# A twelve-layer Perceiver block in one program: a bias moved from GpSimd to ScalarE, weight splitting moved to two other layers, and one pair of weight loads put behind one more wait

## The reference

```python
# L0 attention (l0a below): 16 heads of 128, causal
# L0 feed-forward (l0f): Hadamard transforms around a gated MLP of 1024
# L1 attention (l1a): a state-space layer; for each row
v1, v2 = (v[..., 0::2], v[..., 1::2])       # v is B + B_bias, and C + C_bias, 64 heads x 64
c, s = (jnp.cos(phi), jnp.sin(phi))
r1 = v1 * c - v2 * s
r2 = v1 * s + v2 * c
# L2 feed-forward (l2f): mixture of experts, the two best of 8 by softmax score
# L3 cross-attention (l3x): fp8-rounded inputs against fp32 weights
y = jnp.clip(x.astype(jnp.float32) / scale, -FP8_MAX, FP8_MAX)   # then rounded to bf16, to fp8
q = _fp8_linear_pertensor(ln_out, wq, wq_scale, q_in_scale)      # also wk, wv, wqx
out = jnp.einsum('bsi,oi->bso', catq, wproj) * (proj_in_scale * proj_w_scale)
```

## Time and profile before

| | us |
|---|---|
| runs before (three) | 3519.94, 3521.09 (median), 3527.53 |
| the profiled execution | 3520.92 |
| its span in the profile | 3519.1 |
| PE busy | 2822.5 (80% of the span) |
| DVE busy | 2205.2 (63%) |
| ACT busy | 1477.5 (42%) |
| POOL busy | 755.1 (21%) |
| l0a | 410 to 757 |
| l0f | 757 to 889 |
| l1a | 1050 to 1507 |
| l2f | 2085 to 2254 |
| l3x | 2254 to 2925 |
| GpSimd idle within a round, l0f / l2f | 30.0 to 32.9 / 33.3 to 34.2 |
| a quarter of wproj in l3x, from issue to landing (median) | 8.8 |

### The profile page before, as it was taken

The page is one execution under the profiler, slowest core; times in us unless marked ns, Lnnn a source line. Parts: engine busy times, 40 slices in busy tenths (PEclk is TensorE's granted clock), DMA queues, the critical chain, the costliest instruction groups (busy, mean ns, idle before and its releaser), DMA issues. The chain is left out here.

```text
span 3519.1 us, 63930 instructions
## 1 busy us (share of the span) xinstructions
PE 2822.5 (80%) x24148; PEld 2008.9 (57%) x24148; DVE 2205.2 (63%) x4685; ACT 1477.5 (42%) x3000; POOL 755.1 (21%) x1074
## 2 busy tenths in 40 slices
PE   6777699978777788857998759788788886888687
PEld 3333387867664556534655336455555565777576
DVE  6999644542558888866565643376676774433764
ACT  4899611111446464534443113255455541332223
POOL 5222177400002232211111001121111112322100
PEclk8889799999887776758999879899889997999798
DMA  3999933200010000010000241112211124000000
GB/s 119 199 205 204 208 138 104 86 24 1 15 54 8 3 3 2 2 74 10 6 6 7 75 112 44 39 40 102 84 75 75 75 101 159 1 1 1 1 1 13
DMA packets 340727, 217.82 MB, mean 62 GB/s; under 512 B 298139, under 2 KB 318875, under 8 KB 332833
## 3 DMA queue, kind: packets, MB, share of 16 engines
q1 hardware_dynamic: 332260, 214.49, 22.3%
q10 hardware_dynamic: 8256, 0.52, 0.2%
HBM read 127.95 MB, written 18.87 MB: 42 GB/s over the span
## 5 line engine op out<-in xcount | busy, mean ns | idle before, releaser
L1252 ACT ACTIVATE l0x_pb<-l0x_ex,l0x_neg_max,l0x_q_scale 128x2048 uint16<-128x2048 f32 x128 | 267.1, 2088 | 36.5 <-POOL l0x_neg_max L1355 27.7
L1151 PE MATMUL l0x_s_ps<-l0x_kT,l0x_qT 128*128 128x512 bf16 x512 | 179.4, 443 | 76.1 <-DVE l0x_ex L1450 39.2
L1448 DVE TENSOR_SCALAR_CACHE_REDUCE l0x_ex<-l0x_s_ps 128x1024 f32<-128x1024 f32 x128 | 156.2, 1220 | 14.5 <-PE l0x_s_ps L1151 13.7
L1450 DVE TENSOR_SCALAR_CACHE_REDUCE l0x_ex<-l0x_s_ps 128x1024 f32<-128x1024 f32 x128 | 156.1, 1220 | 1.0 <-PE l0x_s_ps L1151 1.0
L264 PE MATMUL l3x_bank<-l3x_w_kv_x,l3x_ctxT 128*128 128x512 f32 x256 | 127.4, 644 | 8.4 <-ACT l3x_ctx_k L766 4.6
L1151 PEld LDWEIGHTS l0x_s_ps<-l0x_kT,l0x_qT 128*128 128x128 bf16 x512 | 35.0, 103 | 156.5 <-DVE l0x_ex L1450 104.0
L1161 PEld LDWEIGHTS l0x_o_ps<-l0x_v,l0x_vT 128*128 128x128 f16 x2048 | 71.5, 99 | 55.8 <-DMA l0x_vT<-l0x_pb 25.3
L2315 PEld LDWEIGHTS l1a_bank<-l1a_u,l1a_gm 64*64 64x64 f32 x2048 | 95.3, 193 | 13.5 <-issue 12.7
L2315 PE MATMUL l1a_bank<-l1a_u,l1a_gm 64*64 64x8 f32 x2048 | 98.0, 234 | 3.4 <-DVE l1a_gm L2671 3.3
L2307 PE MATMUL l1a_bank<-l1a_r,l1a_r 32*64 32x64 f32 x2048 | 72.6, 282 | 31.7 <-DVE l1a_r L2653 28.0
L3782 PE MATMUL l3x_bank<-l3x_wproj,l3x_cat 128*128 128x256 bf16 x768 | 90.8, 276 | 7.9 <-DVE l3x_cat L3668 7.9
(11 more groups left out here) (775 smaller groups left out, 7688.1 us busy)
## 6 DMA issues: line engine op xcount, KB each, us to landing
l3x_wproj<-l3x_wproj_parts SPq DMA_DIRECT2D x32, 1536.0 KB, 8.8
l3x_wproj_parts<-l0a_parts SPq DMA_DIRECT2D x24, 256.0 KB, 2.9
l0a_raw<-in_L_xattn_wproj SPq DMA_DIRECT2D x8, 512.0 KB, 4.5
l3a_w<-in_L_attn_W SPq DMA_DIRECT2D x4, 1024.0 KB, 11.4
l3x_wq_parts<-l0a_parts SPq DMA_DIRECT2D x12, 256.0 KB, 3.0
l3x_wqx_parts<-l0a_parts SPq DMA_DIRECT2D x12, 256.0 KB, 2.4
l3x_wq<-l3x_wq_parts SPq DMA_DIRECT2D x1, 3072.0 KB, 10.2
l3x_wqx<-l3x_wqx_parts SPq DMA_DIRECT2D x1, 3072.0 KB, 12.9
```

The costliest lines, as they stand in the source:

```text
L1151: ins = mm(s_ps[:, j * 512:(j + 1) * 512], qT[:, h, :], kT[:, h // 2, j * 512:(j + 1) * 512], start=True, stop=True)
L1252: s.activation(pb[:, h % 4, :], ex[:, h % 4, :], ACT.Exp, scale=q_scale[:, h:h + 1], bias=nb[:, h:h + 1], accum_out=sums[:, h:h + 1]).then ...
L1448: v.tensor_scalar(ex[:, h % 4, 0:1024], s_ps[:, 0:1024], 1.0, None, ALU.mult, ALU.max, accum_out=low_max[:, h:h + 1]).then_inc(o.up(scores ...
L1450: v.tensor_scalar(ex[:, h % 4, 1024:2048], s_ps[:, 1024:2048], 1.0, None, ALU.mult, ALU.max, accum_out=high_max[:, h:h + 1]).then_inc(o.up ...
```

## The change

Three edits.

One. `WeightParts` takes the projections or the output weights alone. The 12 chunks of the projections are now divided in l0f, three in each of its four rounds, behind the norms; the 8 chunks of wproj in l2f, two in each round, behind the second softmax power. SP's loads and stores move along: three chunks are asked for ahead of `load_next`, and the stores follow behind it. Layer l0a has none of it any more, and its GpSimd loop is a hardware loop.

Two. In l1a the bias of B is added by ACT, 16 instructions of 128x128 for each half, just ahead of C's; GpSimd adds none.

Three. In l3x SP waits for `kc1.filled` of the next tile as well before it issues quarters 0 and 1.

```diff
@@ WeightParts
-    def __init__(self, L, d):
+    def __init__(self, L, d, projections=(), output=False):
...
-        for kind, name in enumerate(("wq", "wk", "wv", "wqx")):
+        for kind, name in projections:
...
-        for n in range(8):
+        for n in range(8 if output else 0):
@@ l0a, SP and GpSimd
-            parts.load_first(sp)
             load_next(sp, env)
-            parts.store_all(sp)
...
-            for t in range(TILES - 1):
-                for j in range(3 * t, min(3 * t + 3, len(parts.chunks))):
-                    parts.divide(pool, j)
+            with pool.Fori(0, TILES - 1) as t:
                 o = Order(pool, L.order["pool"], t)
                 o.t = t + 2
                 whole(norm.pool(o))
@@ l0f, SP and GpSimd
+        parts = WeightParts(L, env.dram, projections=enumerate(("wq", "wk", "wv", "wqx")))
...
+            parts.load_first(sp)
             load_next(sp, env)
+            parts.store_all(sp)
...
-            in_turn(*(tile["gpsimd"](pool, 0) for tile in tiles))
-            with pool.Fori(1, TILES // 2) as t:
+            for t in range(TILES // 2):
                 in_turn(*(tile["gpsimd"](pool, t) for tile in tiles))
+                for j in range(3 * t, 3 * t + 3):
+                    parts.divide(pool, j)
@@ l1a, ACT
-            def biased_c(o, half):
-                for e, dst in enumerate((v1[1], v2[1])):
-                    for k in range(half * NG // 2, (half + 1) * NG // 2):
-                        last = e and k == (half + 1) * NG // 2 - 1
-                        s.activation(dst[:, k, :], vt[:, 2 + e, :], ACT.Identity, bias=bc_bias[:, 2 + e, k:k + 1]).then_inc(o.up(c_biased if last else None), 1)
+            def biased(o, half):
+                for n, biased_n in enumerate((b_biased, c_biased)):
+                    for e, dst in enumerate((v1[n], v2[n])):
+                        for k in range(half * NG // 2, (half + 1) * NG // 2):
+                            last = e and k == (half + 1) * NG // 2 - 1
+                            s.activation(dst[:, k, :], vt[:, 2 * n + e, :], ACT.Identity, bias=bc_bias[:, 2 * n + e, k:k + 1]).then_inc(o.up(biased_n if last else None), 1)
@@ l1a, GpSimd
-            def biased_b(o, half):
-                ks = slice(half * NG // 2, (half + 1) * NG // 2)
-                pool.wait_ge(vt_ready.sem, vt_ready.value(o.t))
-                if o is not first:
-                    pool.wait_ge(roped.sem, roped.value(o.t - 1, 3 if half else 1))
-                for e, dst in enumerate((v1[0], v2[0])):
-                    g_.tensor_tensor(dst[:, ks, :], vt[:, e, :].unsqueeze(1).broadcast_to([P, NG // 2, P]),
-                                     bc_bias[:, e, ks].unsqueeze(2).broadcast_to([P, NG // 2, P]), ALU.add).then_inc(o.up(b_biased if e else None), 1)
...
-                    for half in range(2):
-                        biased_b(o, half)
@@ l2f, SP and GpSimd
+        parts = WeightParts(L, env.dram, output=True)
...
+            parts.load_first(sp)
             load_next(sp, env)
+            parts.store_all(sp)
...
                 in_turn(*(tile["gpsimd"](pool, t) for tile in tiles))
+                for j in range(2 * t, 2 * t + 2):
+                    parts.divide(pool, j)
@@ l3x, SP
                     sp.wait_ge(y_ps.sem, y_ps.value(t))
+                    sp.wait_ge(kc1.filled.sem, kc1.filled.value(t + 1))
                     quarters(0, 1)
```

More of the change, by code:

```diff
@@ L1538, in load_first @@
     def load_first(self, sp):
-        sp.dma_start(self.scale[:], self.scale_src).then_inc(self.scale_loaded, 16)
+        if self.chunks[0][2]:
+            sp.dma_start(self.scale[:], self.scale_src).then_inc(self.scale_loaded, 16)
         for j in range(self.BUFFERS):
@@ L1606, in l0_attn @@
         y_ps, tile_done, x_biased = L.sig("y_ps"), L.sig("tile_done", primed=True), L.sig("x_biased")
-        parts = WeightParts(L, env.dram)
         block = L.block()
@@ L2464, in _ @@
             for half in range(2):
-                biased_c(first, half)
+                biased(first, half)
                 sines(first, half)
@@ L2484, in tile @@
                     act.wait_ge(roped.sem, roped.value(t, 1))
-                    biased_c(o, 0)
+                    biased(o, 0)
                     sines(o, 0)
                     act.wait_ge(roped.sem, roped.value(t))
-                    biased_c(o, 1)
+                    biased(o, 1)
                     sines(o, 1)
@@ L2541, in _ @@
             odd_steps_of(first, 1)
-            for half in range(2):
-                biased_b(first, half)
             def tile(t, more):
```

## The result

The changed kernel takes 3565.8 us in the median of four runs (3560.6 to 3570.7), against 3520.5 before: ratio 1.0123, 95% interval 1.0107 to 1.0140. Its profiled execution has a span of 3564.3 us, 45.2 over that of before. By stages, in us, from GpSimd's first layer norm (L231) of a layer to that of the next; l3x is counted from the norm named `l3x_ln`, 2.3 us behind its first.

| | before | after | difference | forecast |
|---|---|---|---|---|
| l0a | 331.2 | 314.1 | -17.1 | -16.5 |
| l0f | 133.2 | 149.2 | +16.0 | +14 |
| l1a | 478.6 | 543.8 | +65.2 | +60 |
| l2f | 171.2 | 187.4 | +16.2 | +28 |
| l3x | 665.1 | 625.6 | -39.5 | -54 |

The account below looks back on a forecast made before the run. No one engine was taken to bound the program, so each edit was priced in its own stage: -16.5 + 14 + 28 + 60 - 54 = +31.5 on 3520.9, giving 3552 us. Its own range was 3535 to 3569, the overall range 3509 to 3580.

Parts of the forecast that it names:

- the 3.5 taken from the first tile: l0a: of the first tile's 8.9 us over, 3.5 were expected back when splitting is taken out.
- The chain of the alternation: l0f, first round: 14 VectorE instructions alternate with GpSimd's, setup ends 22 us later where 6.3 were free: +14.
- 6 us, and 1 more for the clock: l2f: cost of a round from VectorE's held routing instructions and the clock behind idle time; 4 x 7 = +28.
- Six instructions were counted as held: l2f, second tile's routing: six of ten small VectorE instructions each wait for GpSimd, 7 to 9.5 us together.
- The step in VectorE's and ScalarE's chain: l1a: ScalarE's added 9.1 us a tile less 0.7 slack, less 1.1 from a quicker L2562: +7.3 a tile.
- 9 and one tile's 7.3: l1a: 9 us for the first tile's 32 added instructions, 7.3 for each of seven loop tiles; +60 in all.
- no issue time before L964: l3x: sign that the forecast is right, VectorE's issue wait of 7.04 us in a loop tile gone.
- Gain 45.1 + 6 x 1.3 = 53: l3x: L927's whole wait goes and six tiles' stretch to L820 shortens by 1.3 each; with 1 more, -54.
- The sentence on the Trainium skill's rule: l3x: a taken branch out of the window makes a DMA fetch, so part of the wait stays after the change.
- Rival B: VectorE's small and setup instructions not held by GpSimd: l0f +2, l2f 0, total 3512, faster; chance 0.14.
- Rival D: l1a's longer ScalarE run is absorbed: l1a +8 to +17, total about 3505; chance 0.06.
- Rival C: Quarters don't hold the fetch, or it meets them elsewhere: l3x gains 0 to half, 3579 to 3606; chance 0.12.

Follow-up runs that it names:

- run four: Kernel before with only the splitting moved to l0f and l2f, GpSimd also waiting there for VectorE's down weights and first expert product: 3516.7 us, ratio 0.9978.
- run two: Kernel before with one edit, quarters 0 and 1 of the next tile in l3x also waiting for kc1.filled: 3487.8 us, ratio 0.9894.
- run five: Kernel before with only quarter 1 in l3x waiting for kc1.filled, quarter 0 loaded where it was: 3508.4 us, ratio 0.9949.
- run six: Kernel before with VectorE's loop over tiles in l3x written out, so no jump back, quarters loading where they did: 3474.6 us, ratio 0.9860.
- run three: Kernel before with one edit, the splitting of the weights moved from l0a to l0f and l2f: 3539.5 us, ratio 1.0046.
- run eight: Kernel before with C's bias for the second half of the groups in l1a added by GpSimd, not ScalarE: 3534.1 us, ratio 1.0023.
- run nine: Kernel before with quarters later, one chunk left in l0a, eleven in l0f and eight in l2f behind VectorE's work, B's bias on GpSimd: 3469.1 us, ratio 0.9841.
- run ten: Kernel before with quarters later, splitting mostly moved behind VectorE's work, B's bias on GpSimd, and VectorE's l3x loop written out: 3460.7 us, ratio 0.9816.
- run seven: Kernel before with ScalarE adding B's bias in l1a for the second half of the groups only, GpSimd the first: 3553.1 us, ratio 1.0087.
- run one: Kernel before with one edit, B's bias in l1a on ScalarE and none on GpSimd: 3585.6 us, ratio 1.0184.

## Why the prediction was right, and where its sizes were off

The sign, the range and the mechanisms held: 3565.8 measured, 3552 forecast, in the forecast's own range of 3535 to 3569. That the total is so near is in part luck. Two stages were off by more than 10 us, one each way: l2f cost 12 less than forecast, and l3x gained 14.5 less. With only the error of l3x and those of l1a and l3a the total would have been about 3576, outside that range.

- l0a, -17.1 for -16.5: right, even the 3.5 taken from the first tile.
- l0f, +16.0 for +14: right. The chain of the alternation came as worked out: 14 instructions held, the setup 21 us later within its stage (22 forecast), and 15.1 of the 16 us are in the first round. Run four shows that the alternation is the cause: without it the setup is as short as before, and of its +8 in l0f 5.8 come from three chunks that begin behind the setup and end too late for the next norm.
- l2f, +16.2 for +28. The step that failed in size is "6 us, and 1 more for the clock" a round; it was 4.0. Six instructions were counted as held, each for 1.2 to 1.6 us. Four were, for 0.14, 1.76, 0.71 and 1.94 us; the two that came right behind a held one (L623, L628) went through. L681 came 4.1 to 4.6 us later in its round, and not 6 to 8. The cause is shown: run four takes the cost away by the order alone.
- l1a, +65.2 for +60. The step in VectorE's and ScalarE's chain was right: L2550 did take 0.55 us for 1.41, and VectorE waits for the scale. A loop tile is 7.7 us longer in the mean of six (6.6 to 8.3) and not 7.3; the first L2705 comes 18.2 us later, where 9 and one tile's 7.3 were forecast, and the last tile adds 1.3. Most of the excess is a wait that wasn't in the sum. The copy to vt comes 8.25 us behind dt_raw in the mean of seven tiles (8.23 in the tile shown, 1312.21 to 1320.44), and came 7.7 behind it before. VectorE stands idle between them for TensorE's L2308 in five of these tiles, for 0.4 to 2.0 us, before in two, for 0.4 and 0.6. TensorE's granted clock over l1a was 0.69 for 0.72; that this is why TensorE is late was not tried.
- l3x, -39.5 for -54. The cause was right, by runs two, five and six. One of the signs did not come: "no issue time before L964" held in all but two tiles. The step that was mis-sized is "Gain 45.1 + 6 x 1.3 = 53": it took the whole wait as gone and the last tile's 17.6 us from L927 to L820 as what a loop tile would get. 8.4 us of the wait stayed, since the fetch behind the jump takes time even with the quarters out of its way (run six). And the stretch shortened by 2.7 us in all and not by 8. TensorE's low clock did go: L927 takes 1.06 us for 1.94, and the granted clock from 2534 to 2560 is 1.00. But TensorE now waits 2.2 us in the stretch for ScalarE's rows (L759, four waits of 0.16 to 0.74), and ScalarE waits 2.8 and 2.6 us there for the keys' means, which VectorE and GpSimd make. With the jump gone the wait is 0 and the stretch 18.0 (2452.92 to 2470.95) in each of the six tiles; that is 45.1 and 7.6 us less, less 1.4 of small waits for ScalarE, the 51 of run six. The sentence on the Trainium skill's rule, "Runtime: NRT & Kernel Launch", section "Instruction fetch mechanics", had said that part of the wait stays; the traces agree, with 1.4 us a tile.
- l3a, +4.0, was not forecast. The instructions are the same, and TensorE is busy 279.0 us for 275.3 in it; 3.1 of the 4.0 are in its last 100 us, where the granted clock was 0.93 for 0.95, and 0.9 in a stretch of 50 us, with 0.85 for 0.90. Runs two to six and eight to ten had 336 to 338.5 in l3a, run seven 333, run one 331. What sets this is open. It needn't be the change: there is one profile of the kernel before, and beside the experiments that kernel took 2 to 4 us more than in it.

Rival B (small instructions not held) is refuted by the rows of l2f, and run four agrees; two of its six did go through. Rival D (ScalarE's run absorbed) is refuted by run one, and run seven shows that the cost counts from the first 16. Rival C (the quarters don't hold the fetch) is refuted by runs two and six. The Trainium skill's rule that a DMA never contends with a compute engine ("SBUF — State Buffer", section "Who interferes with whom") is not contradicted: what the loads put off was the fetch of instructions, itself a DMA transfer, and not an engine's access. The same section's rule on two SBUF inputs was shown at 128x1024 (3.14 us for 1.22), and at 128x8 by L630 (0.88 for 0.17).

## What to carry to other kernels

Before giving work to an idle GpSimd, look at what VectorE does at the same moment. Here its instructions with two SBUF inputs, and a TENSOR_SCALAR on SBUF, were held; a wait that puts GpSimd's work a few us later took away a cost of 16 us in l2f at no price. Before moving work to an engine that is busy 55% of the time, look for whether it has a wait at all between the copy that starts its run and the result that ends it: here there was 0.27 us of it, and 9.4 us of added work a tile cost 65 us in eight tiles. And where an engine has idle time of kind "issue" right behind its loop's start, look at which DMA transfers are issued just then, and for packets of the kind "instruction" right behind them: move the transfers, or write the loop out.

## What the runs showed of the hardware that was not expected

A small VectorE instruction that is ready as a GpSimd instruction ends gets through, though GpSimd's next one begins 0.07 us later. In the tile shown the start tells the two kinds apart: L628 starts 0.13 us ahead of GpSimd's instruction and takes its own 0.28 us; L632 starts 0.02 us ahead of one and takes 2.17 for 0.23, until that one has ended.

A jump back to a loop's start cost several instruction fetches of 8 KB, one after the other (22 fewer in the program without VectorE's jumps in l3x), and VectorE waited for two of them. They can stand behind different transfers: with one quarter in the way the wait before L964 is as long as with two (6.5 us a tile for 6.7), and the one before L966 all but gone (0.4 for 3.75). With no quarter in the way the fetch still cost TensorE 1.4 us a tile.
